# One tower kernel, another lead: row maxima computed 60 steps ahead of the scores instead of 96, and a new order for the work that shares one PSUM bank

## The reference, cut to what matters

```
h = h + attention(layernorm(h))      # 8 heads of 16 channels, softmax over 746 keys
h = h + ffn_top1(layernorm(h))       # router, expert e: relu(x W1[e] + b1[e]) W2[e] + b2[e]
```

## Time and profile before

| | before |
|---|---|
| median of three runs | 1410.22 us |
| the profiled execution | 1411.15 us |
| its span, first to last instruction | 1409.1 us |
| PE busy | 1259.2 us, 89% |
| DVE busy | 1093.6 us, 78% |
| ACT busy | 968.1 us, 69% |
| POOL busy | 594.4 us, 42% |
| mean granted TensorE clock | 0.95 |

### The profile page before, as it was taken

One profiled execution on the slowest core, in us unless ns is written; L12 is line 12 of the kernel. 1 busy time (PEld: TensorE's weight loads), 2 busy tenths in 40 slices (PEclk: granted clock), 3 DMA queues, 4 the chain that ended last, 5 costly groups with the idle time before them and its releaser, 6 DMA issues.

```text
span 1409.1 us, 54650 instructions
## 1 busy us (share of the span) xinstructions
PE 1259.2 (89%) x21768; PEld 780.5 (55%) x21768; DVE 1093.6 (78%) x3006; ACT 968.1 (69%) x2479; POOL 594.4 (42%) x544
## 2 busy tenths in 40 slices
PE   6377999999999999999999999999999862999996
PEld 3123546454555555555555455555555431989996
DVE  8368898888888888888888888888889313667775
ACT  5212878787878778787878787877767850667774
POOL 1122424343444536353434344453621222556664
PEclk9558999999999999999999999999999985999999
DMA  7145041423325050404142232505040502333331
GB/s 174 42 57 100 19 84 43 83 66 60 78 48 104 21 120 21 107 36 90 48 78 69 57 82 44 110 15 121 21 107 3 159 24 68 94 88 103 106 104 51
DMA packets 70383, 102.51 MB, mean 73 GB/s; under 512 B 14828, under 2 KB 59875, under 8 KB 69710
## 3 DMA queue, kind: packets, MB, share of 16 engines
q1 hardware_dynamic: 60992, 78.68, 25.2%
q0 software_dynamic: 8416, 20.22, 5.1%
q10 hardware_dynamic: 762, 0.55, 0.1%
HBM read 60.96 MB, written 39.00 MB: 71 GB/s over the span
## 4 chain that ended last, share of the span: by engine, by line
PE 63%; DVE 14%; ACT 11%; issue 5%; DMA 4%; POOL 2%; SPq 1%; another core or an unknown queue 0%; POOLq 0%; ACTq 0%; DVEq 0%
PE psum L977 30%; PE psum L1052 11%; DVE half_max L850 10%; PE psum L982 7%; PE psum L1106 6%; PE psum L1116 6%; ACT arena L605 5%; DMA arena<-in_x_t_dram 2%; ACT q_full L593 1%; ACT k_full L593 1%; DMA k_rows<-k_parts_dram 1%; SPq L399 1%; ACT k_part L593 1%; PE psum L996 1%; PE psum L1097 1%
## 5 line engine op out<-in xcount | busy, mean ns | idle before, releaser
L850 DVE TENSOR_REDUCE half_max<-psum 128x1 f32<-128x373 f32 x1536 | 773.6, 538 | 143.3 <-PE psum L977 134.4
L605 ACT ACTIVATE arena<-psum 128x373 f32<-128x373 f32 (+1 forms) x1536 | 667.3, 487 | 248.6 <-PE psum L977 241.6
L977 PE MATMUL psum<-k_rows,arena 96*32 96x373 bf16 x6144 | 525.5, 332 | 27.4 <-DMA k_rows<-k_parts_dram 15.5
L977 PE MATMUL psum<-arena,k_rows 98*32 98x373 bf16 x6144 | 513.1, 325 | 12.6 <-ACT arena L605 11.6
L1052 PE MATMUL psum<-arena,values 128*32 128x373 f32 (+1 forms) x3072 | 314.0, 476 | 1.5 <-ACT arena L605 1.2
L977 PEld LDWEIGHTS psum<-k_rows,arena 96*32 96x32 bf16 x6144 | 180.2, 97 | 182.6 <-DVE half_max L850 90.4
L977 PEld LDWEIGHTS psum<-arena,k_rows 98*32 98x32 bf16 x6144 | 177.8, 95 | 158.4 <-ACT arena L605 67.5
L503 POOL DMA_INDIRECT routed_rows_dram<-rows,pos_i x96 | 96.2, 1002 | 338.2 <-DVE tok_id L844 247.1
L543 POOL DMA_INDIRECT out_dram<-arena,slot_id x102 | 122.8, 1204 | 88.0 <-issue 52.1
L1052 PEld LDWEIGHTS psum<-arena,values 128*32 128x32 f32 (+1 forms) x3072 | 99.9, 110 | 27.4 <-issue 1.9
L527 POOL TENSOR_TENSOR rstd<-var_eps,minus_half 128x6 f32<-128x6 f32 x16 | 21.5, 1347 | 203.1 <-DVE var_eps L727 203.1
(11 more groups left out here) (155 smaller groups left out, 1442.5 us busy)
## 6 DMA issues: line engine op xcount, KB each, us to landing
arena<-q_parts_dram SPq DMA_DIRECT2D x192, 93.2 KB
k_rows<-k_parts_dram SPq DMA_DIRECT2D x192, 93.2 KB
arena<-routed_rows_dram SPq DMA_DIRECT2D x102, 130.0 KB
q_parts_dram<-q_part SPq DMA_DIRECT2D x16, 559.5 KB, 3.2
k_parts_dram<-k_part SPq DMA_DIRECT2D x16, 559.5 KB, 3.2
arena<-in_x_t_dram SPq DMA_DIRECT2D x3, 703.1 KB, 17.6
seq<-in_w_dram SPq DMA_DIRECT2D x1, 2048.0 KB, 10.3
seq<-in_w_dram SPq DMA_DIRECT2D x8, 256.0 KB, 5.8
```

What stands on the lines that cost most here:

```text
L605: nc.scalar.activation(probs[0:kn(kt), G % N_P, j, :], st_bank[s % N_ST][0:kn(kt), 0:HALF], ACT.Exp).then_inc(s_exp, 1)
L850: nc.vector.tensor_reduce(half_max[:, s:s + 1], mx_bank[s % N_MX][:, 0:HALF], AX.X, ALU.max)\
L977: last = nc.tensor.matmul(dst[n:n + m], weights[:, n:n + m], moving, start=start, stop=stop)
```

## The change

`LEAD` = 60: at step s of body i the maximum tile is now tile s+60 of sample i while s is under 36, and tile s-36 of sample i+1 after that. So body -1 begins maxima only at step 36, and body 15 still has maxima in its steps 0 to 35. The last tile of a sample (95) falls on step 35 and tile 47 on step 83. The fills get another order: MAX1 moves from step 1 to step 38 and MAX0 from step 61 to step 86 (the last one); the others shift by up to 9 steps (V's first half from 64 to 73). In the SP queue MAX0's rows now go behind the load of heads 0 to 3 instead of ahead of it.

```diff
+    LEAD = 60
-        FILLS = (("MAX1", 0, 1), ("HTOK", 0, 4), ("HTOK", 1, 7), ("OT0", 0, 11), ("OT0", 1, 15), ("OT1", 0, 19),
-                 ("MT", 0, 22), ("OT1", 1, 25), ("PROJ", 0, 29), ("MT", 1, 32), ("PROJ", 1, 36), ("XNT", 0, 39),
-                 ("XNT", 1, 42), ("Q", 0, 45), ("Q", 1, 49), ("K", 0, 53), ("K", 1, 57), ("MAX0", 0, 61), ("V", 0, 64),
-                 ("XN2T", 0, 67), ("XN2T", 1, 70), ("LOGIT", 0, 73), ("V", 1, 77), ("RANK", 0, 85))
+        FILLS = (("HTOK", 0, 1), ("HTOK", 1, 4), ("OT0", 0, 8), ("OT0", 1, 12), ("OT1", 0, 16), ("MT", 0, 20),
+                 ("OT1", 1, 23), ("PROJ", 0, 27), ("MT", 1, 30), ("PROJ", 1, 34), ("MAX1", 0, 38), ("XNT", 0, 41),
+                 ("XNT", 1, 44), ("Q", 0, 47), ("Q", 1, 51), ("K", 0, 55), ("K", 1, 59), ("XN2T", 0, 64),
+                 ("XN2T", 1, 67), ("LOGIT", 0, 70), ("V", 0, 73), ("V", 1, 77), ("RANK", 0, 81), ("MAX0", 0, 86))
+        def maximum_of(i, s):
+            return (i, s + LEAD) if s + LEAD < STEPS else (i + 1, s + LEAD - STEPS)
...
     # sp: body
+                if live(i, 2):
+                    if live(i, 0):
+                        sp.wait_ge(s_st, scores(i, STEPS // 2 - 1))
+                    sp.wait_ge(s_qk_w, (i + 2) * 32 + 32)
+                    load_group(par, 0)
                 if live(i, 1):
                     sp.wait_ge(s_free, fill(i, "MAX0", 0))
                     for n in range(2):
                         sp.dma_start(q_rows[1 - par][KR + n:KR + n + 1, 0:GH, 0:L],
                                      max_rows[0][GH * n:GH * (n + 1), :]).then_inc(s_mrow, 16)
-                if live(i, 2):
-                    if live(i, 0):
-                        sp.wait_ge(s_st, scores(i, STEPS // 2 - 1))
-                    sp.wait_ge(s_qk_w, (i + 2) * 32 + 32)
-                    load_group(par, 0)
...
     # act: body
-                    if s == 2 and live(i, 0):
+                    if s == 39 and live(i, 0):
                         max_out(i, i, 1, "MAX1")
-                    if s == 62 and live(i, 1):
+                    if s == 87 and live(i, 1):
                         max_out(i, i + 1, 0, "MAX0")
...
     # dve: body
-                    if live(i, 1):
-                        dve.wait_ge(s_mx, (i + 1) * STEPS + (s + 1))
-                        nc.vector.tensor_reduce(half_max[:, s:s + 1], mx_bank[s % N_MX][:, 0:HALF], AX.X, ALU.max)\
+                    b, m = maximum_of(i, s)
+                    if 0 <= b < B:
+                        dve.wait_ge(s_mx, b * STEPS + (m + 1))
+                        nc.vector.tensor_reduce(half_max[:, m:m + 1], mx_bank[m % N_MX][:, 0:HALF], AX.X, ALU.max)\
                           .then_inc(s_red, 1)
-                        if s % 48 == 47:
-                            maxima(i + 1, s // 48)
+                        if m % 48 == 47:
+                            maxima(b, m // 48)
...
     # pe: body
-                    if live(i, 1):
-                        b, h, t, half = i + 1, s // 12, s % 12 // 2, s % 2
-                        if s % 48 == 0:
-                            pe.wait_ge(s_ld[s // 48], b * 192 + 192)
+                    b, m = maximum_of(i, s)
+                    if 0 <= b < B:
+                        h, t, half = m // 12, m % 12 // 2, m % 2
+                        if m % 48 == 0:
+                            pe.wait_ge(s_ld[m // 48], b * 192 + 192)
```

More of the change, by code:

```diff
@@ L615, in body @@
                               .then_inc(s_o, 1)
-                    if s == 2 and live(i, 0):
+                    if s == 39 and live(i, 0):
                         max_out(i, i, 1, "MAX1")
-                    if s in (5, 8) and live(i, 2):
-                        part = s // 8
+                    if s in (2, 5) and live(i, 2):
+                        part = s // 5
                         wait(act, s_ln_p, (i + 2) * 3)
                         copy_out(i, "HTOK", part, h_cur[:, 3 * part:3 * (part + 1), :].rearrange("p t d -> p (t d)"))
-                    if s in (23, 33) and live(i, -1):
-                        part = s // 33
+                    if s in (21, 31) and live(i, -1):
+                        part = s // 31
                         copy_out(i, "MT", part, merged_t[:, 3 * D * part:3 * D * (part + 1)])
-                    if s in (40, 43) and live(i, 2):
-                        part = s // 43
+                    if s in (42, 45) and live(i, 2):
+                        part = s // 45
                         copy_out(i, "XNT", part, xn_t[:, 3 * D * part:3 * D * (part + 1)])
[L629 to L632, removed]
-                    if s == 62 and live(i, 1):
+                    if s in (48, 49, 52, 53) and live(i, 2):
+                        q_or_k(i, "Q", (s - 48) // 4, (s - 48) % 4)
+                    if s in (56, 57, 60, 61) and live(i, 2):
+                        q_or_k(i, "K", (s - 56) // 4, (s - 56) % 4)
+                    if s == 87 and live(i, 1):
                         max_out(i, i + 1, 0, "MAX0")
-                    if s in (68, 71) and live(i, -1):
-                        part = s // 71
+                    if s in (65, 68) and live(i, -1):
+                        part = s // 68
                         copy_out(i, "XN2T", part, xn2_t[:, 3 * D * part:3 * D * (part + 1)])
-                    if s == 83 and live(i, -1):
+                    if s == 79 and live(i, -1):
                         act.wait_ge(s_rt, (i - 1) * 10 + 7)
@@ L867, in body @@
                         norm_rows(nc.vector, lambda t: xn[:, t, :], lambda t: h_cur[:, t, :], mv, rstd, s_ln_p)
-                    if s in (30, 37) and live(i, -1):
-                        residual(i, i - 1, s // 37)
+                    if s in (28, 35) and live(i, -1):
+                        residual(i, i - 1, s // 35)
                     if 38 <= s < 44 and live(i, -1):
@@ L880, in body @@
                         split(dve, nc.vector, s_apart_v, i, "K")
[L881 to L886, removed]
+                    if 71 <= s < 79 and live(i, -1):
+                        router(i, i - 1, s - 71)
+                    if 80 <= s < 82 and live(i, -1):
+                        router(i, i - 1, s - 72)
+                    if 82 <= s < 88 and live(i, -1):
+                        ranks(i, i - 1, s - 82)
             run_bodies(dve, body)
@@ L1068, in body @@
                              q_rows[par][0:KM, h, qh * HALF:(qh + 1) * HALF]).then_inc(s_st, 1)
[L1069 to L1076 removed]
+                    b, m = maximum_of(i, s)
[3 more added lines that the diff above has]
+                            pe.wait_ge(s_ld[m // 48], b * 192 + 192)
+                        wait(pe, s_red, b * STEPS + (m + 1 - N_MX))
+                        quad(mx_bank[m % N_MX][:, 0:HALF], q_rows[b % 2][0:KR, h, D * t:D * (t + 1)],
+                             k_rows[b % 2][0:KR, h, half * HALF:(half + 1) * HALF]).then_inc(s_mx, 1)
                     for n, after in enumerate(WEIGH_AT):
```

12 lines of the change are left out of this document (6 added, 6 removed).

## The result

The changed kernel takes 1406.7 us in the median of 20 runs (1402.1 to 1410.4), the kernel before 1410.6 in 20 runs beside them (1407.0 to 1415.9). The ratio is 0.997, with an interval of 0.9957 to 0.9982: faster by 0.3%, a little more than what can be told from no change. The forecast was 1399. Its profiled execution took 1402.19 us. That is 9.0 less than the 1411.15 of the profiled execution before, so the profile shows twice the gain that the medians do.

The account below looks back on a forecast made before the run. Bounds: start waits, then PE narrowly ahead of DVE in inner bodies (DVE leads late), ACT in body 15. From 1411.15, -18.3 + 5.0 - 4 + 4.5 = -12.8 gave 1398.4 profiled; median forecast 1399, range 1386 to 1413.

Parts of the forecast that it names:

- Start: Up to body 0's first score: XNT comes five steps after the first maximum, -18.3 us, bounds -23 to -15.
- rival E: At the start, POOL's norm or the read-back sets the K chain; only part of 18.3 comes, 1406 to 1409; chance 0.07.
- MAX0's rows: At body boundaries, a new wait for rows queued behind the read-back: 0.3 us at each of 15, +4.5, bounds 0 to +20.
- rival B: At body boundaries, MAX0's rows become a wait in every body, 1.3 us each: 1414 us; chance 0.14.
- Late steps, boundary, middle: Inner bodies: together -0.3 us a body, over 15 bodies about -4, bounds -18 to +6.
- middle: Steps 35 to 43: DVE has more work than PE, about +0.9 us a body, bounds 0 to +1.6.
- Late steps and boundary: Steps 71 to 87 and boundary: PE loses about 0.2 us to DVE instead of 1.4, -1.2 a body.
- Tail: Body 15: maxima in 36 of its steps make it longer, +5.0 us, bounds +4 to +6.5.

Follow-up runs that it names:

- rows_first: Changed kernel with MAX0's row DMAs ahead of the read-back in every body: 1399.56 us, ratio 0.9929 to the kernel before.
- rows_first_twice: Changed kernel with MAX0's row DMAs ahead of the read-back only in bodies -1 and 0: 1397.35 us, ratio 0.9911 to the kernel before.
- same_60: Changed kernel with MAX0's rows first in bodies -1 and 0, lead 60, rerun in the one-session comparison: 1372.16 us, ratio 0.9857 to before.
- same_66: Changed kernel with MAX0's rows first in bodies -1 and 0 and lead 66, in the one-session comparison: 1364.93 us, ratio 0.9809 to before.
- stats_later: `rows_first` with the second layer norm's statistics at steps 46 to 51 in place of 38 to 43: 1405.45 us, ratio 0.9965 to before.
- again2: The changed kernel unaltered, a single traced execution on another chip: 1406.2 us.
- again: The changed kernel unaltered, timed and traced once more: 1404.39 us, ratio 0.9966 to the kernel before.

## Why the prediction was wrong in size

**Start: right.** -18.3 was forecast, with a first score at 114.4; it came at 113.0 in the mean. XNT follows the first maximum after 2.5 us, not 39 steps later, and rival E is refuted. The wait for MAX0's rows at body 0, which I had put into this term, was there with 3.68 us.

**Body 0: not in the sum.** It lasts 4.1 us longer, counted from the score that runs. I had priced PE's lower clock level only as a bound of the start and let body 0 follow at its old length. But that level now covers 5.0 to 9.6 us of it where it covered 3.2: about 2.1 us in the mean, by the same estimate.

**MAX0's rows: wrong in place.** I took "0.3 us for each of 15 boundaries, +4.5". At body 1's it is 1.2 to 2.1 us. At the 14 others it is nothing in the first trace; in the repeats PE's weight loads wait for the rows at two to four of them, up to 1.0 us, and its matmuls once, 0.3 us. I had priced all from body 12, where the write of K comes 14.3 us before the end (972.41 - 958.10). Body 0 has no output projection and no second norm; it lasts 61 us where an inner body lasts 65, and PE was at its end 12.4 us after the write at 161.59. POOL's split, the write, the twelve reads and then the rows took as long as ever: 13.9 us from that write to the landing at 175.53. At the inner boundaries there is slack, and undoing the order there wins nothing (`rows_first`), so rival B fell. In the profiled executions the term is thus 3 us too large. In the medians it was too small, together with the wait at body 0 that I had accepted as a price of the start: `rows_first_twice` and `same_60` win 7.0 and 8.4 us and nearly all of the spread. With it the time is 12.5 us below the kernel before (0.9911 of 1410): what I forecast for the change itself is reached once these two waits are gone.

The Trainium skill, "DMA: Bandwidth & Descriptors", section "Queues, rings and completion order", says that a semaphore increment lands only after every earlier write of the same DMA engine. The traces agree as far as they go: behind twelve reads PE was released 4.98 and 4.62 us after the pair's first issue (108.24 to 113.22, 170.95 to 175.57), while the pair ahead of them was seen within 2.95 us of its own. They don't show whether the increment waited for the reads' writes or the rows' own data did. And the later issue by SP, 2.4 us at body 0, is a cost beside this rule.

**Late steps, boundary, middle: the step of the sum that failed.** "-0.3 a body, over 15 bodies about -4" came as +2.0 over bodies 1 to 14, 6 us on the other side: the largest miss. The period went from 65.24 to 65.45. The two terms can be told apart, since both kernels make the same number and kinds of fills from step 16 to 78, with one MAX fill among them, and likewise from step 78 over the boundary to step 16. In means over bodies 2 to 13, the middle went from 42.48 to 43.12 us, +0.6 where +0.9 was forecast. Late steps and boundary went from 22.77 to 22.29, -0.5 where -1.2 was forecast, and this is the term that failed. In the faster condition the two are +0.1 and 0.0.

The forecast had PE lose 1.4 us a body to DVE before and 0.2 after. Before, the fill's matmuls stood behind `max_parts` for 9.2 us in 13 bodies, 0.7 a body. After, they stand at step 83 behind `next_row` for 5.9 us in 14 bodies, 0.4 a body, and at step 35 behind `rows` for 3.5 us in 15, so that the waits of the MAX fills sum to what they had been. I had set DVE's total over steps 71 to 83 against PE's and found them equal. That sum leaves out that the fill needs `next_row` or `rows` to free the bank, and that the three small instructions come ahead of it in the same step. Leads of 62 and 66 leave the total of steps 71 to 83 as it is and only move the three instructions within it; they win 0.2 and 0.45 us a body, and 0.6 in the faster condition (64.47 in `same_60` to 63.84 in `same_66`, median bodies). But nearly all of that lies at step 35 (steps 36 to 48: 8.45 us in `same_60`, 7.87 in `same_66`) and so belongs to the middle; steps 78 to 88 stay (6.50 and 6.59). Why the late steps gave so much less than 1.2 is therefore shown only in part: the wait came back at step 83, but taking it away alone wins nothing there. My range for the two terms, -18 to +6, held it. The three small instructions were most of the middle's cost (0.6 a body), and the statistics, which I had at 2.0 of 7.6 us, a small part (0.2 in `stats_later`).

**Tail: the number right, with luck.** +5.0 was forecast and +5.6 measured, but the 5.0 were to lie before step 36 of body 15. Steps 0 to 36 took 3.2 us longer (20.66 to 23.91), below the bound of +4. Steps 36 to 88 added 1.0, and the last eight steps 3.0 (4.11 to 7.1), which the forecast didn't have; from there to the first read of routed rows it was 1.7 us shorter. In the faster condition the sum is +3.7, with 2.2 before step 36.

**What stays between the profile and the medians.** The stretches sum to -8.1 us in the mean of four traces. Against the forecast's -12.8 that is a start 1.5 better, body 0 worse by 4.1, the inner bodies by 2.0 and the tail by 0.6 (the forecast's terms for rows and middle had summed to +0.5). The medians have -3.9. Two of the three repeats were taken, like the first, near the lower end of the changed kernel's 1402 to 1410; the slower one, `again2`, lies 3.3 us later by body 14, of which 2.0 are there by body 1. That the two row waits carry most of the spread is shown by `rows_first_twice` and `same_60`. Which part of the DMA chain varies was not traced.

**What stays open.** Why the gain is 4 to 6 us in the one condition and 10.6 in the other. In the traces the difference is placed: in bodies 1 to 14 (+2.0 against -0.3) and in body 15. There the changed kernel's last eight steps, with PE idle before scores for which the trace names no releaser, took 7.13 us, against 4.11 before, in the first condition, and 2.88 in both kernels in the second. The timeline of PE in the first condition and then in the second:

```profile
1138.22 0.34 PE L983 MATMUL psum<-arena,k_rows 98*32 98x373 bf16 x4 [0.37 <-issue]
1139.75 0.34 PE L983 MATMUL psum<-arena,k_rows 98*32 98x373 bf16 x4 [1.19 <-issue]
```

```profile
1125.57 0.34 PE L983 MATMUL psum<-arena,k_rows 98*32 98x373 bf16 x4 [0.32 <-ACT arena L610]
```

So in the slower condition PE meets short idle times of its own, up to 1.19 us, that the changed kernel's trace in the faster one doesn't show; a kernel that waits less for DVE is exposed to more of them. That last clause is argued from differences, not shown.

## What to carry to other kernels

Price a boundary wait in the shortest body that has it, not in a typical one: a chain of write, read and rows has a fixed length, and the body that leaves out work is the one that arrives early. A small transfer moved behind a large one costs where the consumer is next in line; here it had to be moved back in two bodies, worth 7 to 8 us and the spread, and moving it back in all was worth less. When a reduction's last small instructions get a new step, look at what stands beside them in that engine's program and at which of these the next fill waits for, not only at the engine's sum over the stretch: six steps of lead gave 7 us. And a wait that disappears from the list is not yet a gain: the one for `next_row` did, and its steps took as long as before.

## What the runs showed of the hardware

The same kernels, on two of the same chips, ran at 1410 us in the first sessions and at 1390 in the later ones, with the same granted clock (0.950 before, 0.955 and 0.956 after the change). In an inner body of the kernel before the difference is 0.7 us, all of it in steps 0 to 16 and 16 to 36 (12.7 and 13.2 us against 11.4 and 13.9); in the changed one 0.9 to 1.0. With the condition, what the change is worth goes from 0.3% to 0.8%. The clock fell at 106.7 before PE's wait at body 0 had begun and stayed down for 7.1 us of full work behind it, and in `rows_first_twice`, with no wait there at all, for 10.0. The shorter wait at body 1 was followed by 3.4 us at the lower level in one execution (`again`) and by none in the three others traced. And an instruction of DVE that took 0.20 us alone took up to 0.84 us beside one of POOL, in 13 of 13 meetings ending 0.06 us after it (`stats_later`).
